# Query and key projections on a PSUM bank each, the first chunk's scores ahead of their second halves, three output biases on VectorE, and a new order of the work

## The chip, the cores and the metric

One core of one Trainium2 chip. The metric is the device time of the kernel in microseconds, the median of three runs. Every time below is in microseconds unless it says ns.

## What is computed

A batch of 32 sequences (B) of 64 tokens (L) with 256 features (D). All of it is float32. Cut to what matters, with the names of the code:

```
y   = x @ Wc[id].T + bc[id]                       # per sequence, 8 subjects
q,k,v = y @ Wq.T + bq, y @ Wk.T + bk, y @ Wv.T + bv    # 16 heads of 16
sim = q k^T / sqrt(16) / (|temperature| + 0.1)    # 64 x 64 per head
s   = sum over 5 frequencies of alpha * sin(2 pi sim / f + phi)
w   = sigmoid(s) / (sum over keys + 1e-10)
o   = (w v) @ Wo.T + bo;  o = layernorm(o) * gamma + beta
x1  = x + o
x2  = layernorm(x1 + relu(x1 @ W1[lang] + b1) @ W2[lang] + b2) * g[lang] + b[lang]
# recurrence over the 32 sequences, its batch the 64 token rows, 256 wide:
c   = sigmoid(f) * c + sigmoid(i) * tanh(g)       # gates from x2 and c
out = x1 + tanh(x2 @ wo.T + c_final @ uo.T + bo)
```

## The kernel before

All engines run lists of calls written out by hand, one list for each engine. Semaphores tie them together. No engine ever takes a later call ahead of an earlier one, so the order of each list sets what a wait holds up.

**Attention.** The 32 sequences are five groups g of 4, 8, 8, 8 and 4. `condition` (L419) makes y, `turn_tokens` transposes it, `conditioned` on VectorE (L1435) adds the bias. `queries` and `keys` (project, L407) make q and k in two chunks c of 128 features (eight heads). Before, chunk c of both q and k goes to PSUM bank c of `pf`: `keys(g, c)` waits on TensorE until ScalarE has copied `queries(g, c)` out (L955). The first chunk of group 0's queries is masked into `qm` by VectorE and ScalarE. All others are spread into it by SP, with eight DMAs each (`spread_q`, L286). `scores` (L479) makes a tile of scores in a bank of `pf`, and `copy_scores` (L982) carries it to SBUF.

The score rows are then worked on in 32 units n. `angle(n, f)` scales a unit for one of five frequencies into int32, partly on VectorE (L1459), partly on ScalarE (L991). `wrap(n)` (L1468, VectorE) takes it modulo a turn. `sines(n)` (L1000, ScalarE) takes all five sines. `add_sine(n, f)` (L1481, L1483, VectorE) sums them with alpha. `weights(n)` (L1006, ScalarE) is the sigmoid. `weighted(n)` (L497, TensorE) multiplies with the values, and `divided(m)` (L1496 to L1500, VectorE) divides two units by their sums. A flag on `sines` and `weights` says that the activation table is to be loaded first (L997, L1004).

**The rest, by eight parts q of four sequences.** `turned`, `output_projection` (L514 the bias as a matmul of a row of ones, L516 the product, weights centred by `centre_output_weights`, L1408 to L1418, so that the mean is zero), `squares` on ScalarE (L1015), a root on GpSimd (L362, L365), `residual` and `residual_added` on VectorE (L1525, L1532), `turn_residual`, `adapter_down` (L530), `hidden` (L1537), `adapter_up` (L538), `base`, `adapted` (L1550), `moments`, the root again, `normalise`, `turn_normed`, `modulated` (L1580) and `shifted_language` (L1586), which makes z ready for the recurrence. SP loads each part's own weights with 13 DMAs (`load_rest`).

**The recurrence.** Step n: `input_gates` (L555) and `state_gates` (L562) on TensorE, `gates` on ScalarE (L1032, then the bias of step n + 2 at L1028), `cell_step` on VectorE (L1591 to L1596), `state_turned` on TensorE (L568), `state_copy` on VectorE (L1601). At the end `state_output`, `output_kept`, `output_part` and `output_sum` gather the eight results, which go through a tanh, a sum and a DMA each.

Of the kernel before, what the change touches and what calls it, by code (L numbers as in the profile page):

```python
# [21 lines left out]
P = 128  # L22
# [55 lines left out]
MASKED_BY_DVE = 5  # L78
BY_PE = (0, 1, 2, 6, 7)
# [34 lines left out]
def build(nc, x_in, xt_in, ids_in, small_in, cond_in, down_in, up_in, up_b_in, rows_in, bo_in, wq_in, wk_in, wv_in, bv_in, wo_in,  # L114
          gate_w_in, gate_u_in, gate_b_in, c0_in, c0t_in, wout_in, uout_in, eye_in, out):
    with ExitStack() as ctx:
# [21 lines left out]
        rows = sb("rows", [P, 3, D])  # L138
# [72 lines left out]
        mask_ready, qm_dve, qm_act = sem("mask_ready"), sem("qm_dve"), sem("qm_act")  # L211
# [45 lines left out]
        def _(sp):  # L257
# [53 lines left out]

            load_cond(1, 1)
            load_cond(1, 0)
# [3 lines left out]
            load_cond(1, 3)  # L317
# [4 lines left out]
            load_cond(2, 2)  # L322
            load_x(2)
            spread_q(1, 1)
            load_cond(2, 3)
            load_cond(2, 1)
            load_rest(1)
            load_cond(3, 1)
            load_cond(3, 3)
            load_cond(3, 2)  # L330
            spread_q(2, 0)
            spread_q(2, 1)
            load_x(3)
            load_rest(2)
            load_cond(3, 0)
            load_x(4)
            load_cond(4, 0)
            load_cond(4, 1)
            spread_q(3, 0)
            load_rest(3)  # L340
            load_rest(4)
            spread_q(3, 1)
# [61 lines left out]
        def _(pe):  # L404
            def project(dst, w, src, oc, n, sem):
                for kc in range(KC):
                    mm = pe.matmul(dst[:, oc, 0:n], w[:, kc, oc * P:(oc + 1) * P], src[:, kc, 0:n],  # L407
                                   start=(kc == 0), stop=(kc == KC - 1))
                mm.then_inc(sem, 1)
# [26 lines left out]
            def queries(g, c):  # L436
                pe.wait_ge(y_ready, g + 1)
                if g == 0:
                    pe.wait_ge(qk_s, 32)
                project(pf, wq, yT, c, SIZES[g] * L, q_done)  # L440

            def keys(g, c):
                pe.wait_ge(q_ready, g * KC + c + 1)
                project(pf, wk, yT, c, SIZES[g] * L, k_done)

            def values(q, h):
# [5 lines left out]
                pe.wait_ge(s_copied, FIRST[g] + SIZES[g] // 2)  # L452
                pvw = pf[:].rearrange("p c (b n) -> p (c b) n", n=P)
# [7 lines left out]
            def scores(n):  # L461
# [3 lines left out]
                if t == 0:  # L465
                    pe.wait_ge(k_ready, g * KC + KC)
# [42 lines left out]
            def output_projection(q, j):  # L509
# [68 lines left out]
            def output_kept(q, j):  # L578
                pe.wait_ge(go_kept, q + 1)
                pe.wait_ge(s_copied, B)  # L580
                pe.wait_ge(att_ready, B // 2)
# [18 lines left out]

            for _ in range(8):
# [9 lines left out]
            queries(0, 1)  # L611
            keys(0, 0)
            keys(0, 1)
# [3 lines left out]
            scores(1)  # L617
            values(0, 0)
# [8 lines left out]
            queries(1, 0)  # L627
            queries(1, 1)
            keys(1, 0)
# [3 lines left out]
            scores(4)  # L633
            scores(5)
            scores(6)
            scores(7)
            weighted(2)
            weighted(3)
            turned(0)
# [18 lines left out]
            adapter_up(0)  # L658
            queries(2, 1)
            keys(2, 0)  # L660
            weighted(4)
            weighted(5)
            turn_normed(0)
            keys(2, 1)
            weighted(6)
            input_gates(0, 0)
            weighted(7)
            input_gates(0, 1)
            input_gates(1, 0)
            state_gates(0)  # L670
            input_gates(1, 1)
            output_part(0, 0)
            output_part(0, 1)
            scores(12)
            scores(13)
            state_turned(0)
            scores(14)
            input_gates(2, 0)
            scores(15)
            state_gates(1)  # L680
            values(3, 0)
            values(3, 1)
            values(4, 0)
            weighted(8)
            weighted(9)
            values(4, 1)
            weighted(10)
            weighted(11)
            input_gates(2, 1)
            input_gates(3, 0)  # L690
            input_gates(3, 1)
            state_turned(1)
            scores(16)
            scores(17)
            turned(1)
            turned(2)
            state_gates(2)
            output_projection(1, 0)
# [3 lines left out]
            output_projection(2, 0)  # L702
            condition(5, 0)
            condition(5, 1)
            condition(6, 0)
            condition(6, 1)
            turn_residual(1)
            output_projection(2, 1)
            state_turned(2)
            adapter_down(1)  # L710
            turn_tokens(3)
            adapter_up(1)
            state_gates(3)
# [3 lines left out]
            turn_normed(1)  # L717
            queries(3, 1)
            input_gates(4, 0)
            state_turned(3)  # L720
            keys(3, 0)
            input_gates(4, 1)
            state_gates(4)
            input_gates(5, 0)
            keys(3, 1)
            turn_residual(2)
            state_turned(4)
            input_gates(5, 1)
            adapter_down(2)
            state_gates(5)  # L730
            weighted(14)
            weighted(15)
            input_gates(6, 0)
            adapter_up(2)
            input_gates(6, 1)
            state_turned(5)
            scores(20)
            scores(21)
            state_gates(6)
            weighted(16)  # L740
            input_gates(7, 0)
            scores(22)
            turn_normed(2)
            state_turned(6)
            input_gates(7, 1)
            state_gates(7)
            scores(23)
            input_gates(8, 0)
            state_turned(7)
            output_part(1, 0)  # L750
            input_gates(8, 1)
# [1368 lines left out]
```

## Time and profile before

| | us |
|---|---|
| median of 3 runs | 362.87 (362.35 to 364.96) |
| the profiled execution's own time | 366.25 |
| its span | 364.5 |
| TensorE, VectorE, ScalarE busy | 305.0, 299.4, 278.6 |
| mean granted TensorE clock, of full speed | 0.963 |

The profile is of one execution, so durations and waits are taken from it. Busy time is not a bound by itself: the stages have different limits. The rows that count are in the section ahead of the prediction. In them a form in brackets behind a row is idle time of that engine just ahead of the row, with what ended it; "issue" stands for time in which nothing the profile shows was waited for. TensorE shows each float32 matmul as two records, so "x8" is four matmuls.

### The profile page before, as it was taken

The page shows a single profiled execution, that of the slowest core. Times are in us where ns is not written, and L with a number is a line of the kernel's source. Part 1 is how long each engine was busy: PE and PEld are TensorE (multiplying, and loading weights), DVE is VectorE, ACT ScalarE, POOL GpSimd, SP SyncE. Part 2 cuts the span into 40 slices and gives each one's busy share as a digit, 9 for nine tenths or more (in the row PEclk, how much of TensorE's full clock was granted, in tenths as well). Part 3 has the DMA queues.
Part 4 walks back from the last instruction along what each step waited for, and adds up shares of the span by engine and source line. Part 5 has one row for each costly group of instructions (what it writes and reads, how often), then busy time and mean ns, then how long its engine had stood idle before and what let it go on. Part 6 is the DMA issues. An engine that isn't in the chain of part 4 may idle for free.

```text
span 364.5 us, 6732 instructions
## 1 busy us (share of the span) xinstructions
PE 305.0 (84%) x2316; PEld 171.6 (47%) x2316; DVE 299.4 (82%) x661; ACT 278.6 (76%) x407; POOL 29.9 (8%) x42
## 2 busy tenths in 40 slices
PE   6947687476898799989888998999987988998895
PEld 5735346244444645534445545444544543543353
DVE  2378974849999999999899999899998999764344
ACT  1387789859999999999989999698995886222223
POOL 6000000001100002220200002000001110101000
PEclk9998699969999789999999999899999999999999
DMA  6448444562610640244123100000332031000006
GB/s 186 154 128 249 178 79 114 153 172 67 182 22 8 137 93 28 55 111 97 31 72 64 14 2 0 2 13 7 77 97 73 3 81 37 3 0 0 2 8 222
DMA packets 31078, 27.52 MB, mean 76 GB/s; under 512 B 11588, under 2 KB 25028, under 8 KB 31045
## 3 DMA queue, kind: packets, MB, share of 16 engines
q1 hardware_dynamic: 30756, 26.58, 27.7%
q10 hardware_dynamic: 288, 0.53, 0.5%
q8 instruction: 18, 0.29, 0.4%
q14 instruction: 16, 0.12, 0.1%
HBM read 23.02 MB, written 2.10 MB: 69 GB/s over the span
## 4 chain that ended last, share of the span: by engine, by line
DVE 48%; PE 20%; issue 11%; ACT 9%; SPq 7%; POOL 2%; DMA 2%; DVEq 0%; ACTq 0%
DVE sc L1483 16%; DVE ang L1468 7%; PE pg L562 4%; DVE ang L1459 4%; PE pf L479 3%; PE pg L555 3%; ACT ang L991 3%; DVE sc L1481 2%; PE pf L407 2%; DVE vz L1449 2%; SPq L286 1%; ACT ang L1000 1%; DVE fc L1591 1%; POOL rs L362 1%; PE pr L573 1%
## 5 line engine op out<-in xcount | busy, mean ns | idle before, releaser
L1483 DVE SCALAR_TENSOR_TENSOR sc<-ang,small,sc 128x512 f32<-128x512 f32 (+1 forms) x160 | 98.2, 639 | 1.5
L1000 ACT ACTIVATE ang<-ang,qs 128x2560 f32<-128x2560 int32 x32 | 77.4, 2426 | 2.6 <-DVE ang L1468 2.3
L991 ACT ACTIVATE ang<-sc,phase 128x512 int32<-128x512 f32 (+1 forms) x126 | 73.3, 642 | 0.3 <-DVE sc L1483 0.2
L555 PE MATMUL pg<-gate_w,zT 128*64 128x384 f32 x256 | 53.5, 520 | 3.3 <-DVE zT L1586 3.3
L1468 DVE TENSOR_SCALAR ang<-ang 128x2560 int32<-128x2560 int32 x32 | 47.4, 1485 | 6.9 <-ACT ang L991 6.7
L562 PE MATMUL pg<-gate_u,cT 128*64 128x384 f32 x256 | 49.0, 504 | 4.0 <-DVE cT L1601 4.0
L479 PE MATMUL pf<-qm,kT 128*64 128x256 f32 x256 | 35.2, 420 | 13.2 <-issue 11.6
L1032 ACT ACTIVATE gat<-pg 128x384 f32<-128x384 f32 x32 | 15.5, 485 | 29.2 <-PE pg L562 28.8
L479 PEld LDWEIGHTS pf<-qm,kT 128*64 128x64 f32 x256 | 19.9, 150 | 25.9 <-issue 16.4
L1459 DVE TENSOR_SCALAR ang<-sc,phase 128x256 int32<-128x256 f32 (+1 forms) x74 | 27.4, 411 | 4.3 <-ACT sc L982 4.3
L562 PEld LDWEIGHTS pg<-gate_u,cT 128*64 128x64 f32 x256 | 16.9, 139 | 25.8 <-issue 16.0
L982 ACT ACTIVATE sc<-pf 128x512 f32<-128x512 f32 x32 | 18.2, 588 | 10.8 <-PE pf L479 10.7
L555 PEld LDWEIGHTS pg<-gate_w,zT 128*64 128x64 f32 x256 | 15.9, 140 | 21.9 <-issue 15.4
L497 PEld LDWEIGHTS pav<-vz,sc 128*64 128x64 f32 x512 | 18.4, 143 | 13.4 <-ACT sc L1006 9.3
L497 PE MATMUL pav<-vz,sc 128*64 128x34 f32 x512 | 20.4, 230 | 5.0 <-ACT sc L1006 3.6
L1006 ACT ACTIVATE sc<-sc 128x512 f32<-128x512 f32 x32 | 19.5, 623 | 2.6 <-DVE sc L1483 2.4
L407 PE MATMUL pf<-yT,wq 128*128 128x512 f32 (+1 forms) x40 | 17.8, 580 | 3.5 <-DVE yT L1435 3.5
L1591 DVE SCALAR_TENSOR_TENSOR fc<-gat,cst 128x128 f32<-128x128 f32 x32 | 9.1, 283 | 13.0 <-ACT gat L1032 13.0
L362 POOL TENSOR_SCALAR rs<-var 128x2 f32<-128x2 f32 x8 | 3.6, 455 | 185.9 <-ACT x L1015 185.9
L457 PE MATMUL pf<-wv,yT 128*64 128x128 f32 x256 | 16.2, 277 | 2.3 <-ACT sc L982 2.3
L1481 DVE TENSOR_SCALAR sc<-ang,small 128x512 f32<-128x512 f32 (+1 forms) x40 | 16.4, 426 | 1.6 <-ACT ang L1000 1.6
L428 PE MATMUL pf<-wc,xg 128*64 128x256 f32 x128 | 14.9, 381 | 2.6 <-issue 1.9
(124 smaller groups left out, 469.3 us busy)
## 6 DMA issues: line engine op xcount, KB each, us to landing
wc<-in_cond SPq DMA_DIRECT2D x30, 257.0 KB, 3.0
wa<-in_down SPq DMA_DIRECT2D x32, 66.0 KB, 1.9
w<-in_up SPq DMA_DIRECT2D x32, 64.2 KB, 2.2
xt<-in_xt SPq DMA_DIRECT2D x8, 256.0 KB, 3.0
b<-in_up_b SPq DMA_DIRECT2D x32, 64.0 KB, 2.1
out_t<-go SPq DMA_DIRECT2D x8, 256.0 KB, 2.3
xg<-in_x SPq DMA_DIRECT2D x3, 512.0 KB, 5.0
qm<-qT SPq DMA_DIRECT2D x48, 32.0 KB, 2.1
```

The source lines that it names most:

```text
L407: mm = pe.matmul(dst[:, oc, 0:n], w[:, kc, oc * P:(oc + 1) * P], src[:, kc, 0:n], start=(kc == 0), stop=(kc == KC - 1))
L479: mm = pe.matmul(dst[u * L:(u + 1) * L, m * PC * L:(m + 1) * PC * L], kT[:, c, b * L:(b + 1) * L], qm[:, b, u, :, :], start=True, stop=True)
L497: mm = pe.matmul(pav[r, col:col + 2 * HV], at[:, b * L:(b + 1) * L], vz[:, b, p, :, :].rearrange("p u d -> p (u d)"), start=True, stop=True)
L555: pe.matmul(pg[n % 2][u * L:(u + 1) * L, 0:GCOLS], zT[:, q % 2, kc, t * L:(t + 1) * L], gate_w[:, kc, u, :], start=False, stop=(kc == KC - ...
L562: mm = pe.matmul(pg[n % 2][u * L:(u + 1) * L, 0:GCOLS], cT[:, kc, :], gate_u[:, kc, u, :], start=False, stop=(kc == KC - 1), skip_group_ch ...
L991: op = act.activation(ang[:, n % SLOTS, f, r], unit(n)[:, r], ACT.Identity, scale=TURN / FREQS[f], bias=phase[:, p * NF + f:p * NF + f + 1])
L1000: act.activation(a.bitcast(F32), a, ACT.Sin, scale=2 * PI_LOW / TURN, bias=qs[:, 3:4]).then_inc(sine_ready, 1)
L1006: act.activation(unit(n), unit(n), ACT.Sigmoid).then_inc(w_ready, 1)
L1459: op = dve.tensor_scalar(ang[:, n % SLOTS, f, r], unit(n)[:, r], TURN / FREQS[f], phase[:, p * NF + f:p * NF + f + 1], ALU.mult, ALU.add)
L1468: dve.tensor_scalar(a, a, (1 << TURN_BITS) - 1, None, ALU.bitwise_and).then_inc(angle_ready, 1)
L1481: op = dve.tensor_scalar(unit(n)[:, r], sine, amp, None, ALU.mult)
L1483: op = dve.scalar_tensor_tensor(out=unit(n)[:, r], in0=sine, scalar=amp, in1=unit(n)[:, r], op0=ALU.mult, op1=ALU.add)
```

## The change

The projections go to a bank each: every query chunk to bank 0 of `pf`, every key chunk to bank 1. `keys(g, c)` no longer waits for the copy of `queries(g, c)`, and each waits for the copy of its own chunk before. In group 0 the scores of the first chunk (units 0 and 1 of the tiles) stand ahead of `queries(0, 1)` and `keys(0, 1)`, and these wait until both are copied out. The key order within a group is q0, k0, q1, k1. For parts 5, 6 and 7 the bias of the output projection is no longer a matmul: VectorE adds a centred row in PSUM (`output_bias`), behind the projection and ahead of `squares`, which waits for it. The row is loaded as a fourth one of `rows` and centred once by `centre_output_row`. `output_kept` waits for the attention's last division for its bank in `pav` alone. `centre_output_weights` moves on VectorE from ahead of the first angles to behind `divided(1)`. The lists of SP, TensorE, ScalarE and VectorE are reordered throughout. ScalarE's has 24 table loads with a flag where it had 20.

```
+SCORES_FIRST = [True] + [False] * (NG - 1)
+BIAS_BY_DVE = (5, 6, 7)
...
             def project(dst, w, src, oc, n, sem):
                 for kc in range(KC):
-                    mm = pe.matmul(dst[:, oc, 0:n], w[:, kc, oc * P:(oc + 1) * P], src[:, kc, 0:n],
+                    mm = pe.matmul(dst[:, 0:n], w[:, kc, oc * P:(oc + 1) * P], src[:, kc, 0:n],
...
             def queries(g, c):
...
-                project(pf, wq, yT, c, SIZES[g] * L, q_done)
+                wait(pe, q_ready, g * KC + c)
+                if c == 1 and SCORES_FIRST[g]:
+                    pe.wait_ge(s_copied, FIRST[g] + SIZES[g] // 2)
+                project(pf[:, 0, :], wq, yT, c, SIZES[g] * L, q_done)
             def keys(g, c):
-                pe.wait_ge(q_ready, g * KC + c + 1)
-                project(pf, wk, yT, c, SIZES[g] * L, k_done)
+                pe.wait_ge(y_ready, g + 1)
+                wait(pe, k_ready, g * KC + c)
+                project(pf[:, 1, :], wk, yT, c, SIZES[g] * L, k_done)
...
             def values(q, h):
...
                 pe.wait_ge(s_copied, FIRST[g] + SIZES[g] // 2)
+                pe.wait_ge(k_ready, g * KC + KC)
...
             def scores(n):
...
-                    pe.wait_ge(k_ready, g * KC + KC)
+                    pe.wait_ge(k_ready, g * KC + (1 if SCORES_FIRST[g] else KC))
...
             def output_projection(q, j):
...
-                if j == 0:
+                own = q in BIAS_BY_DVE
+                if j == 0 and not own:
                     pe.matmul(pr[:, q % 2, :], ones[:, :], bo[:, :], start=True, stop=True)
...
-                                   start=False, stop=(kc == KC - 1), skip_group_check=True)
+                                   start=(own and j == 0 and kc == 0), stop=(kc == KC - 1), skip_group_check=True)
...
             def squares(q):
                 act.wait_ge(o_done, 2 * q + 2)
+                if q in BIAS_BY_DVE:
+                    act.wait_ge(bias_added, BIAS_BY_DVE.index(q) + 1)
...
+            def centre_output_row():
+
+                dve.wait_ge(rest_s, 16 * len(rest_consts))
+                link(dve.tensor_reduce(rowm[:, :], rows[:, 3, :], mybir.AxisListType.X, ALU.add))
+                link(dve.tensor_scalar(rowm[:, :], rowm[:, :], -1.0 / D, None, ALU.mult))
+                dve.tensor_scalar(rows[:, 3, :], rows[:, 3, :], rowm[:, :], None, ALU.add).then_inc(row_centred, 1)
...
+            def output_bias(q):
+                dve.wait_ge(o_done, 2 * q + 2)
+                dve.wait_ge(row_centred, 1)
+                dve.tensor_tensor(tiles(q), tiles(q), row(3), ALU.add).then_inc(bias_added, 1)
```

On TensorE at the start, behind the transposes of group 0, in the kernel before (wq and wk are the weights of queries and keys, qm the masked queries, wv the values' weights):

```order
L407 MATMUL pf<-yT,wq 128x256 x4
L407 MATMUL pf<-yT,wk 128x256 x4
L615 MATMUL pct<-eye 128x128 x3
L479 MATMUL pf<-qm,kT 64x256 x8
L457 MATMUL pf<-wv,yT 64x128 x16
L479 MATMUL pf<-qm,kT 64x256 x8
```

The same place now:

```order
L410 MATMUL pf<-yT,wq 128x256 x2
L410 MATMUL pf<-yT,wk 128x256 x2
L624 MATMUL pct<-eye 128x128 x3
L487 MATMUL pf<-qm,kT 64x256 x8
L410 MATMUL pf<-yT,wq 128x256 x2
L410 MATMUL pf<-yT,wk 128x256 x2
L465 MATMUL pf<-wv,yT 64x128 x16
```

The second half of both projections has moved behind the first eight matmuls of the scores.

On ScalarE, around the weights of units 8 to 11, before (ang is made by the angles and turned into sines, sc<-sc are the weights, gat the gates, sc<-pf the copies of scores):

```order
L997 ACT_TABLE_LOAD
L1000 ACTIVATE ang<-ang,qs 128x2560
L962 ACTIVATE kT<-pf,small 128x512
...
L1000 ACTIVATE ang<-ang,qs 128x2560
L982 ACTIVATE sc<-pf 128x2x4x64 x2
L1000 ACTIVATE ang<-ang,qs 128x2560
L1004 ACT_TABLE_LOAD
L1006 ACTIVATE sc<-sc 128x512
L991 ACTIVATE ang<-sc,phase 128x512
L1006 ACTIVATE sc<-sc 128x512 x2
```

And now:

```order
L1008 ACT_TABLE_LOAD
L1011 ACTIVATE ang<-ang,qs 128x2560 x2
L1045 ACTIVATE gat<-pg 128x384
...
L1015 ACT_TABLE_LOAD
L1017 ACTIVATE sc<-sc 128x512
...
L1008 ACT_TABLE_LOAD
L1011 ACTIVATE ang<-ang,qs 128x2560
...
L1011 ACTIVATE ang<-ang,qs 128x2560
...
L1015 ACT_TABLE_LOAD
L1017 ACTIVATE sc<-sc 128x512
```

Where the three sines of units 9 to 11 shared one load, and the weights of 8 to 11 another, there are now two loads for each.

On VectorE in the tail, from step 22 of the recurrence, before (fc and cst are a step, cT the state's copy, atq the last division, stage the normed tile, zT the part's z):

```order
L1565 TENSOR_SCALAR stage<-b,mv,rs 128x256 x2
L1580 TENSOR_TENSOR zT<-pr,wa 128x512
L1586 TENSOR_TENSOR zT<-zT,wa 128x512
L1591 SCALAR_TENSOR_TENSOR fc<-gat,cst 128x128
L1593 SCALAR_TENSOR_TENSOR fc<-gat 128x128
L1596 SCALAR_TENSOR_TENSOR cst<-fc 128x128
L1601 COPY cT<-pct 128x128
L1519 TENSOR_TENSOR xt<-xt,rows 128x512
L1525 SCALAR_TENSOR_TENSOR x<-pr,rs,rows 128x256 x2
```

And now:

```order
L1590 TENSOR_SCALAR stage<-b,mv,rs 128x256 x2
L1616 SCALAR_TENSOR_TENSOR fc<-gat,cst 128x128
L1618 SCALAR_TENSOR_TENSOR fc<-gat 128x128
L1621 SCALAR_TENSOR_TENSOR cst<-fc 128x128
L1626 COPY cT<-pct 128x128
L1605 TENSOR_TENSOR zT<-pr,wa 128x512
L1611 TENSOR_TENSOR zT<-zT,wa 128x512
L1544 TENSOR_TENSOR pr<-pr,rows 128x512
L1539 TENSOR_TENSOR xt<-xt,rows 128x512
L1616 SCALAR_TENSOR_TENSOR fc<-gat,cst 128x128
L1618 SCALAR_TENSOR_TENSOR fc<-gat 128x128
L1621 SCALAR_TENSOR_TENSOR cst<-fc 128x128
```

Step 22 has moved behind the normed tile of part 6, and the bias of part 7 (pr<-pr,rows) stands ahead of step 23.

## Rows read from the trace of the kernel before

**Rows 1.** Stages: length; PE, PEld, DVE, ACT, POOL busy (count); clock, DMA share, GB/s

```profile
50.00:81.00 31.00, 19.89 (x208) 13.82 (x206) 19.08 (x35) 24.10 (x37) 0.00 (x0) 0.89 0.55 143
81.00:200.00 119.00, 103.56 (x885) 57.99 (x885) 114.01 (x221) 115.48 (x158) 12.49 (x12) 0.97 0.32 75
200.00:280.00 80.00, 73.78 (x556) 39.75 (x556) 77.00 (x167) 72.14 (x105) 6.32 (x10) 0.98 0.13 31
280.00:309.50 29.50, 25.21 (x197) 12.97 (x199) 27.85 (x79) 21.76 (x35) 2.13 (x4) 1.00 0.17 42
```

**Rows 2.** VectorE's waits, 81 to 309.5: in total, times, longest

```profile
DVE ang L1468 <- ACT ang L991: 5.4, 1, 5.4
DVE stage L1565 <- POOL rs L365: 1.5, 2, 0.9
DVE fc L1591 <- ACT gat L1032: 1.4, 1, 1.4
DVE hT L1537 <- PE pr L530: 1.3, 1, 1.3
DVE cT L1601 <- PE pct L568: 0.7, 1, 0.7
```

**Rows 3.** Timeline of the start (start, duration, engine, line, operation)

```profile
13.60 2.00 PE L407 MATMUL pf<-yT,wq 128*128 128x256 f32 x8 [0.19 <-DVE yT L1435]
16.68 0.68 DVE L1408 TENSOR_REDUCE wom<-wo 128x2 f32<-128x512 f32 x1
18.16 1.95 PE L479 MATMUL pf<-qm,kT 128*64 128x256 f32 x16
18.64 0.47 DVE L1418 TENSOR_SCALAR bo<-bo,bom 1x512 f32<-1x512 f32 x1
20.20 6.16 SPq L286 DMA_DIRECT2D qm<-qT  x8
27.73 3.42 PE L479 MATMUL pf<-qm,kT 128*64 128x256 f32 x16 [4.87 <-issue]
```

**Rows 4.** Group 1: chain of waits, timeline, two stretches (columns as rows 1)

```profile
40.79 3.79 PE pf L407 x4
...
45.47 5.13 SPq L286 DMA_DIRECT2D qm<-qT  x8
60.77 2.07 DVE L1459 TENSOR_SCALAR ang<-sc,phase 128x512 int32<-128x512 f32 x5 [1.61 <-ACT sc L982]
74.22 6.14 PE L479 MATMUL pf<-qm,kT 128*64 128x256 f32 x32 [6.74 <-issue]
...
36.00:38.00 2.00, 0.35 (x3) 0.35 (x4) 1.96 (x6) 2.00 (x5) 0.00 (x0) 1.00 0.99 399
42.00:44.00 2.00, 2.00 (x4) 0.80 (x3) 1.96 (x7) 0.31 (x1) 0.00 (x0) 0.50 0.00 0
```

**Rows 5.** VectorE's groups: count, busy us, mean ns

```profile
L1550 DVE TENSOR_TENSOR b<-pr,b 128x512 f32<-128x512 f32 x8 | 5.4, 680 | 0.0
```

**Rows 6.** Timeline of the tail, TensorE and VectorE

```profile
314.49 1.12 PE L514 MATMUL pr<-bo,ones 1*128 1x512 f32 x2
325.76 0.87 PE L555 MATMUL pg<-gate_w,zT 128*64 128x384 f32 x4
341.12 0.29 DVE L1591 SCALAR_TENSOR_TENSOR fc<-gat,cst 128x128 f32<-128x128 f32 x1 [2.13 <-ACT gat L1032]
344.79 0.29 DVE L1591 SCALAR_TENSOR_TENSOR fc<-gat,cst 128x128 f32<-128x128 f32 x1 [2.13 <-ACT gat L1032]
```

**Rows 7.** Timeline of ScalarE around a table load

```profile
226.28 0.20 ACT L1015 ACTIVATION_READ_ACCUMULATOR x<-pr 128x1 f32 x1
226.50 1.28 ACT L997 ACT_TABLE_LOAD   x1
227.79 2.43 ACT L1000 ACTIVATE ang<-ang,qs 128x2560 f32<-128x2560 int32 x1
```

**Rows 8.** SP's last issue for part 5 (timeline)

```profile
279.51 0.47 SPq L278 DMA_DIRECT2D b<-in_up_b  x1
```

More of the change, by code:

```diff
@@ L617, in _ @@
             scores(1)
+            queries(0, 1)
+            keys(0, 1)
             values(0, 0)
@@ L717, in _ @@
             turn_normed(1)
-            queries(3, 1)
[L719 to L723, printed above, removed]
+            keys(3, 0)
+            turn_residual(2)
+            input_gates(4, 0)
+            input_gates(4, 1)
+            output_part(1, 0)
+            adapter_down(2)
+            state_gates(4)
+            output_part(1, 1)
+            adapter_up(2)
+            queries(3, 1)
+            weighted(14)
@@ L858, in _ @@
+            input_gates(18, 1)
+            state_turned(17)
+            turned(6)
+            adapter_down(5)
+            state_gates(18)
+            adapter_up(5)
+            output_kept(1, 0)
+            output_projection(6, 0)
+            output_projection(6, 1)
+            state_turned(18)
+            weighted(28)
+            input_gates(19, 0)
+            input_gates(19, 1)
+            weighted(29)
             turn_normed(5)
+            state_gates(19)
+            turn_residual(6)
@@ L1078, in _ @@
             angle(0, 3)
+            queries(0, 1)
             angle(0, 4)
-            sines(0, True)
+            keys(0, 1)
             angle(1, 3)
             angle(1, 4)
+            sines(0, True)
+            sines(1, False)
             copy_scores(2)
@@ L1206, in _ @@
             angle(16, 4)
-            sines(15, True)
-            gates(3)
             queries(3, 0)
-            sines(16, False)
+            sines(15, False)
+            residual_turned(2)
+            weights(14, True)
+            keys(3, 0)
             angle(17, 1)
@@ new lines, in _ @@
+            add_sine(21, 3)
+            state_copy(8)
+            add_sine(21, 4)
+            angle(23, 0)
+            angle(24, 0)
+            angle(24, 1)
+            wrap(22)
+            base(3)
+            hidden(3)
+            wrap(23)
+            adapted(3)
+            cell_step(9)
+            wrap(24)
+            divided(10)
+            moments(3)
+            add_sine(22, 0)
+            add_sine(22, 1)
+            state_copy(9)
+            add_sine(22, 2)
+            normalise(3)
@@ L1974, in _ @@
+            hidden(5)
+            add_sine(29, 4)
+            angle(30, 1)
+            angle(31, 0)
+            adapted(5)
+            cell_step(18)
+            moments(5)
+            output_bias(6)
+            wrap(30)
+            normalise(5)
+            state_copy(18)
+            shifted(6)
+            residual(6)
             modulated(5)
-            angle(31, 0)
+            residual_added(6)
             shifted_language(5)
             angle(31, 1)
+            cell_step(19)
```

951 lines of the change are left out of this document (450 added, 501 removed).

## Prediction

> **What bounds the kernel now.** I read the stages first, then VectorE's waits, then the three places where the change moves something. The stages [rows 1] show one long saturated stretch, from 81 to the end of the last sine sum at 309.5. In it VectorE is busy 114.01 + 77.00 + 27.85 = 218.9 of 228.5 us, and ScalarE 115.48 + 72.14 + 21.76 = 209.4. The reader is to see these two columns. So VectorE sets the pace and ScalarE is close behind: 3.5 us idle in the first 119, 7.9 in the next 80, 7.7 in the last 29.5. From 50 to 81 VectorE is idle for 11.9 of 31 us. Behind 309.5 follows a tail of 55 us, in which the recurrence and the chain of the last part run beside each other.
>
> Of VectorE's 9.6 idle us between 81 and 309.5 the waits [rows 2] name 1.5 (for GpSimd's root), 1.4 (gates), 1.3 (the adapter's first product) and 0.7 (the turned state), 4.9 together; three more come to 1.2. The rest, 3.5, is gaps between instructions. (The 5.4 in that view lies ahead of 81.) This is the first bound: work on VectorE there does not shrink, so whatever the new orders do, that stretch can win 6.1 us at most, less what the change adds.
>
> **The start.** Before, both queries, both keys and their four copies stand ahead of the first scores, which begin at 18.16 [rows 3]. Now one projection of each suffices. The row at 13.60 holds both query projections in 2.00, so one less is 1.0, and the keys' likewise. With its own bank the key's first projection runs without waiting for the query's copy, and ScalarE has one query and one key fewer to copy ahead of the scores. ScalarE's masks stay in the way, so I take 0.9 earlier and not more. The second half pays: its queries wait until the first scores are copied out (19.9) and take 1.0, their copy ends at about 21.4. SP's spreading of them began at 20.20 [rows 3]; now it begins at 21.4, and the scores of units 2 and 3, 7.5 behind it before (27.73), at 28.9. That is 1.2 late. VectorE does not notice, since the new order gives it units 0 and 1 whole meanwhile. What follows is a chain: the next group's first query projection (40.79, 3.79 us), its copy, SP's spreading of it (45.47). ScalarE now runs the sines of unit 1 ahead of scores 2, so the token copies that feed this chain are not later, and the vector step ahead of it ends about 0.4 earlier by VectorE's work (two units of 4.2 us from 28.2, then 1.1 and 1.5 us). The granted clock in 42 to 44 is 0.50, that is 1.2 GHz; TensorE had been busy for 0.35 of the 2 us from 36 to 38, ahead of the fall [rows 4]. At 2.4 GHz the projection would take half, 1.9 less. I leave it at the lower level.
>
> From that spreading to the scores of unit 8 at 74.22 SP's queue is full: 28.75 us from 45.47 [rows 4], the same issues in the same number in the new order. ScalarE stands behind those scores with its copies, and VectorE waits 5.4 for it [rows 2]. So all the VectorE idle time before 81 hangs on one number, when 45.47 comes, and I move it by 0.5. VectorE does some more sine sums ahead of the wait now (1.4) and waits some 0.8 longer behind it, for the squares of part 0: 0.6 gained. Term: **-1.1**, of which I count -0.6, since the first half of it stands on ends that I worked out to a few tenths. Ends: -3.0 (the higher clock too) and +1.2 (the late second scores pass on).
>
> The centring of the output weights (16.68 to 19.11, 2.43 us [rows 3]) leaves the gap ahead of the first angles and goes behind the second division. There VectorE waits 1.61 for scores [rows 4], and the division itself comes some 2.5 earlier, since its product now stands ahead of scores 5 to 7. Cost 0; if that cover is gone, 2.4.
>
> **VectorE's added work.** Two of the three biases, for parts 5 and 6, fall before the last sine sum. The nearest operation reads the same PSUM tiles and adds a tile: 680 ns [rows 5], so 1.36. It writes SBUF; nothing here shows one that writes PSUM. Ends 0.5 and 1.2 each; I take 0.68. Centring the bias row is three of the seven instructions of the weights' centring [rows 3], one of them on half the width: 0.7 to 2.4, taken 1.0. One state copy (0.2) goes behind the last sine sum. Term: **+2.2**. TensorE loses three bias products of 1.12 [rows 6], two of them in a stretch where it is not the bound.
>
> **The new orders.** Where they take a wait away it is named: the gates' 1.4, the adapter's 1.3 and the state's 0.7 [rows 2]. Steps 1 to 3 of the recurrence now stand 12 to 28 us of VectorE's work earlier, and steps 4 to 19 have more of other work between them; I count those 3.4 as gone. The 1.5 for the root stays: behind the moments of parts 1 and 2 stand now 1.0 and 1.6 us of other work, before 2.1 and 2.1, and even that did not cover it. Term: **-3.4**.
>
> ScalarE pays for this: 24 table loads in place of 20, one pair more in units 8 to 11 and one in 22 to 25. A load takes 1.28 [rows 7], so four take 5.1. The first pair, 2.6, goes into the stretch up to 200 where ScalarE has 3.5 idle, the second into one with 7.9 [rows 1]. The sines of late units stand 4 to 5 us of ScalarE's work further back, their first sums on VectorE 1 to 2 us further. Ends: 0 (all in idle time) and 5.1 (all passed on). Taken: half of the first pair, nothing of the second. Term: **+1.3**.
>
> Here a rule speaks against the change. Between the accumulator read that ends at 226.48 and the load at 226.50 lies no gap, and the sine starts 0.01 behind the load [rows 7]: a switch costs 1.28. The Trainium skill (ScalarE: Activation LUTs, What ACT_TABLE_LOAD costs) puts a drain of 1.38 us beside each load, 2.66 together. By it the four would be 10.6. The trace disagrees with it, with its 0.02 us.
>
> **The last parts.** The tail has the same ten steps of the recurrence. Part 7 sets its end as much as they do: its normed tile is ready just when step 28 needs it, and from there each step takes 3.67 (341.12 to 344.79 [rows 6]). For part 7 the bias product (1.12) leaves, and a VectorE operation (0.7 and a semaphore) stands between the projection and the squares instead: these start 0.4 earlier. Then the new VectorE order costs: the residual of part 7 stands behind step 23 and its copy, which wait for gates that ScalarE does behind the squares. Counted from the end of the last sine sum, with the durations of before: squares to +8.5, gates 23 to +9.0, step 23 to +9.8, its turned copy to +10.6, residual and sum to +12.15; before that was +11.6. Next hidden(7) to +15.2, state_gates(25) to +16.0, input_gates(26, 0), 0.87 long [rows 6] and now ahead of adapter_up(7), to +16.7, the product to +17.7, the copy of state 25 and the sum of part 7 to +19.0; before +17.3. Step 26 (+21.5) waited for gates before too and takes 1.0 of it up: the normed tile and its two operations (z) end at +24.4, before +23.65. Behind the last step TensorE's work is the same in another order. Term: **+0.7**, ends -0.6 and +2.
>
> **The sum.** -0.6 + 2.2 - 3.4 + 1.3 + 0.7 = +0.2. The profiled execution took 366.25 us (span 364.5 and 1.75 around it), 3.4 above the median of the runs; against its own time the sum is 366.4, and as a difference on the median 362.87 it gives 363.1.
>
> **Rivals.**
> (A) The orders win nearly all that can be won: the 6.1 us of waits go, the loads hide in ScalarE's idle time, and the projection at 40.79 finds the clock at 2.4 GHz (1.9). For it: VectorE's named waits are few, and the recurrence has more room. Against it: ScalarE needs 118 of the 119 us up to 200. -0.6 - 1.9 + 2.2 - 6.1 + 0 + 0 = -6.4: 356.5.
> (B) ScalarE becomes the bound, which is slower. Its four loads all reach VectorE, each as a wait of a first sine sum for its sines, in units 8 to 27. It decides once ScalarE's own idle time between 81 and 280 falls under some 3 us in place of 11.4. Then the gates come late as well and VectorE's waits stay: -0.6 + 2.2 + 5.1 + 0.7 = +7.4: 370.3. With one pair passed on, 367.7. For it: 3.5 idle in 119 is little, and keys(3, 1) and the queries and keys of the last group come 5 to 11 us of ScalarE's work later. Those feed SP: behind scores 28 and 29 SP does the last spreading and then the loads of two parts without a break, to 279.51 [rows 8], and the adapter's wait of 1.3 [rows 2] is for these. If those scores are 2 late, it is 3.
> (C) The orders do nothing: as many waits come as go. -0.6 + 2.2 + 1.3 + 0.7 = +3.6: 366.5.
> (D) A switch stops ScalarE for longer than its load, wherever work is in flight. No row shows it; if each of the four cost its 1.28 twice, that would be 5.1 on top of B, 375.4. The drain of the page named above is such a stop.
>
> **Chances and range.** Around the forecast (359.5 to 366), 0.46; A or most of it, 0.29; B, 0.15; C, 0.08; D, 0.02. A measurement of this kernel can tell about 1%, 3.6 us. Faster than 359.3 is A, 0.29. Slower than 366.5 is B, D and three quarters of C, 0.23. Within is the rest, 0.48. The range takes in A and most of B: 355.5 to 369.5. The forecast's own is 360 to 366.5.
>
> **What would show it.** First scores near 17.3 and those of unit 2 near 29. The scores of unit 8 within 1 us of 73.7. ScalarE's idle time from 81 to 280 at 5 to 8 us; near 2 it is B. VectorE's waits for sines at units 8 to 27 under 2 in sum. The bias additions at 0.7. Steps 22 to 27 of the recurrence within 1 us of 24.2 in all, from the last sine sum on, and 3.67 behind that. I am wrong if the last sine sum ends before 305 or behind 314.

## The result and the profile after

| | us |
|---|---|
| changed kernel, median of 22 runs | 367.94 (363.16 to 369.87) |
| kernel before, median of 22 runs | 363.67 (361.39 to 366.3) |
| ratio | 1.0106 (95%: 1.0083 to 1.0129) |
| profiled execution of the changed kernel, span | 368.23, 366.4 |

The change costs 1.06%, some 3.9 us, just more than what a measurement of this kernel can tell. Ratios leave disturbed runs out, medians don't, so one can say a little more than the other.

One thing has to be known before the traces are compared. The profiled execution of before (366.25) was 2.6 above its median, that of after 0.3 above. So the traces differ by 1.9 us where the runs differ by 4.3.

The stages after, in the columns of [rows 1]:

```profile
50.00:81.00 31.00, 22.66 (x213) 15.76 (x213) 22.86 (x45) 25.36 (x41) 0.93 (x2) 0.83 0.46 132
81.00:200.00 119.00, 101.23 (x884) 58.05 (x880) 113.11 (x216) 117.72 (x153) 6.75 (x10) 0.99 0.27 74
200.00:280.00 80.00, 71.95 (x548) 38.74 (x549) 76.39 (x167) 74.64 (x113) 7.70 (x10) 0.98 0.13 34
280.00:311.50 31.50, 26.06 (x211) 13.40 (x207) 29.61 (x85) 19.81 (x32) 2.59 (x4) 1.00 0.17 45
```

The last sine sum ends at 311.4, before at 309.5. From 81 to there VectorE is idle 11.4 us (230.5 less 219.1), before 9.6. Ahead of 81 it is the other way round: 27.5 idle of 81 (53.46 busy), before 29.4 (51.61 busy). Added up to the last sine sum, VectorE is idle as long as before (38.9 and 39.0), and busy 272.5 in place of 270.5, the size of the added work. ScalarE has 1.3 idle in the first 119 us, before 3.5. VectorE's waits in that stretch, which answer to [rows 2]:

```profile
DVE sc L1494 <- ACT ang L1011: 1.8, 2, 1.1
DVE xt L1539 <- DMA xt<-in_xt: 1.7, 1, 1.7
DVE b L1570 <- DMA b<-in_up_b: 1.5, 1, 1.5
DVE yT L1448 <- PE pf L418: 1.4, 1, 1.4
DVE rden L1509 <- PE pav L505: 0.8, 1, 0.8
DVE stage L1590 <- POOL rs L368: 0.6, 1, 0.6
```

The gates' 1.4, the adapter's 1.3 and the state's 0.7 are gone, as forecast. In their place stand two waits for loads, 3.2 together, and three others, 4.0 together: for sines (1.8), for the condition's turned product (1.4) and for the weighted values (0.8). The chain of waits leads to the loads (start, duration, what; many pieces are left out):

```profile
258.56 1.32 DVE sc L1496 x2
259.88 0.61 DVE zT L1611
264.26 0.76 SPq L279
265.20 0.68 SPq L280
281.76 2.09 DMA b<-in_up_b
283.88 0.69 DVE b L1570
```

The chain of the end runs from VectorE into SP's queue and comes out some 23 us later. SP's rows behind the last spreading, whose issues end at 258.97 (SP's timeline; L275 is the first issue of a part's load):

```profile
260.51 0.40 SPq L275 DMA_DIRECT2D xt<-in_xt  x1
...
271.43 0.59 SPq L275 DMA_DIRECT2D xt<-in_xt  x1
...
281.76 0.47 SPq L281 DMA_DIRECT2D b<-in_up_b  x1
```

The load of part 6 stands ahead of that of part 5, and it overwrites buffers of part 4. It waits for `shifted_language(4)` on VectorE, which ends at 260.48. Before, that step ended at 251.9, six us ahead, and the load of part 6 began at 258.03, when the spreading ended. The load of part 5 needs nothing so late, but stands behind: the end of the loads is at 282.2 in place of 280.0 [rows 8]. VectorE meets it twice (the last column of [rows 5] and here: idle time just ahead):

```profile
274.39 0.69 DVE L1539 TENSOR_TENSOR xt<-xt,rows 128x512 f32<-128x512 f32 x1 [1.69 <-DMA xt<-in_xt]
...
283.88 0.69 DVE L1570 TENSOR_TENSOR b<-x,b 128x512 f32<-128x512 f32 x1 [1.48 <-DMA b<-in_up_b]
```

TensorE at the start, to be held against [rows 3]:

```profile
17.22 1.95 PE L487 MATMUL pf<-qm,kT 128*64 128x256 f32 x16 [0.82 <-ACT kT L973]
19.95 1.10 PE L410 MATMUL pf<-yT,wq 128*128 128x256 f32 x4 [0.79 <-ACT sc L993]
...
29.08 3.68 PE L487 MATMUL pf<-qm,kT 128*64 128x256 f32 x16 [4.16 <-issue]
33.50 5.81 PE L431 MATMUL pf<-wc,xg 128*64 128x256 f32 x32 [0.73 <-issue]
...
42.90 1.98 PE L410 MATMUL pf<-yT,wq 128*128 128x512 f32 x4 [1.32 <-DVE yT L1448]
```

The condition product of group 1 (L431) before:

```profile
31.88 3.68 PE L428 MATMUL pf<-wc,xg 128*64 128x256 f32 x32 [0.73 <-issue]
```

It now takes 2.1 longer, with the granted clock at 0.50 from 28 to 36 (before at 0.51 to 0.63 from 28 to 32, then at full). The query projection behind it begins 2.1 later than before (42.90, before 40.79) and takes 1.98 in place of 3.79, at the full clock. SP's spreading begins at 45.78, before at 45.47.

VectorE's added work is as sized (groups by line):

```profile
L1544 DVE TENSOR_TENSOR pr<-pr,rows 128x512 f32<-128x512 f32 x3 | 2.1, 692 | 0.1
```

### The profile page after: what moved, and what is told of

Same layout as the page of the kernel before. It is cut to its first block, busy times and chain, and to the rows that moved or that the text cites. A ratio compares the mean times of both kernels' runs of the same rounds, so it can differ in the third digit from the quotient of the medians.

```text
span 366.4 us, 6770 instructions
## 1 busy us (share of the span) xinstructions
PE 303.4 (83%) x2310; PEld 172.1 (47%) x2310; DVE 302.7 (83%) x667; ACT 283.8 (77%) x411; POOL 27.0 (7%) x42
## 4 chain that ended last, share of the span: by engine, by line
DVE 47%; PE 18%; ACT 15%; issue 10%; SPq 6%; DMA 2%; POOL 1%; DVEq 0%; ACTq 0%
DVE sc L1496 16%; DVE ang L1481 5%; DVE ang L1472 4%; ACT ang L1002 4%; PE pf L487 4%; ACT ang L1011 3%; DVE sc L1494 3%; PE pg L571 2%; PE pf L431 2%; PE pr L525 2%; DVE fc L1616 1%; PE pf L465 1%; DVE fc L1618 1%; DVE vz L1462 1%; DVE cst L1621 1%
## 5 line engine op out<-in xcount | busy, mean ns | idle before, releaser
L564 PE MATMUL pg<-gate_w,zT 128*64 128x384 f32 x256 | 50.7, 499 | 2.0 <-ACT pg L1041 1.1
L571 PE MATMUL pg<-gate_u,cT 128*64 128x384 f32 x256 | 47.9, 495 | 4.7 <-DVE cT L1626 4.7
L487 PE MATMUL pf<-qm,kT 128*64 128x256 f32 x256 | 36.0, 426 | 12.3 <-issue 7.5
L505 PE MATMUL pav<-vz,sc 128*64 128x34 f32 x512 | 19.6, 227 | 3.0 <-DVE atq L1513 2.3
L465 PE MATMUL pf<-wv,yT 128*64 128x128 f32 x256 | 19.3, 311 | 3.3 <-ACT sc L993 2.1
L410 PE MATMUL pf<-yT,wq 128*128 128x512 f32 (+1 forms) x40 | 16.2, 527 | 4.5 <-DVE yT L1448 3.7
L465 PEld LDWEIGHTS pf<-wv,yT 128*64 128x64 f32 x256 | 17.0, 158 | 6.1 <-ACT sc L993 4.0
L431 PE MATMUL pf<-wc,xg 128*64 128x256 f32 x128 | 17.7, 423 | 2.6 <-issue 1.5
```

Of the source, the lines that this page charges most:

```text
L431: mm = pe.matmul(pft[row:row + L, j, :], xg[:, kc, b * L:(b + 1) * L], wc[:, b, kc * D:(kc + 1) * D], start=(kc == 0), stop=(kc == KC - 1))
L465: mm = pe.matmul(pvw[u * L:(u + 1) * L, b, :], yT[:, kc, b * L:(b + 1) * L], wv[:, kc, u, :], start=(kc == 0), stop=(kc == KC - 1))
L487: mm = pe.matmul(dst[u * L:(u + 1) * L, m * PC * L:(m + 1) * PC * L], kT[:, c, b * L:(b + 1) * L], qm[:, b, u, :, :], start=True, stop=True)
L505: mm = pe.matmul(pav[r, col:col + 2 * HV], at[:, b * L:(b + 1) * L], vz[:, b, p, :, :].rearrange("p u d -> p (u d)"), start=True, stop=True)
L564: pe.matmul(pg[n % 2][u * L:(u + 1) * L, 0:GCOLS], zT[:, q % 2, kc, t * L:(t + 1) * L], gate_w[:, kc, u, :], start=False, stop=(kc == KC - ...
L571: mm = pe.matmul(pg[n % 2][u * L:(u + 1) * L, 0:GCOLS], cT[:, kc, :], gate_u[:, kc, u, :], start=False, stop=(kc == KC - 1), skip_group_ch ...
```

## The experiments

Every ratio is to the kernel before, run on the same chip in turn. A per cent is 3.6 us.

**1. The SP pair and the bias work.** After the traces there were two accounts of the loss: VectorE's added 2.1 us (theory W), or the loads (theory Q). The first run leaves the bias of parts 5 to 7 with TensorE:

```diff
-BIAS_BY_DVE = (5, 6, 7)
+BIAS_BY_DVE = ()
```
and without `output_bias` and `centre_output_row` on VectorE.

> The changed kernel with the bias product of all parts back on TensorE; VectorE's three bias additions and the centring of the row are gone. Theory W (the slowdown is VectorE's added work, 2.1 us up to the last sine sum, in a stretch that VectorE bounds): 2.1 to 2.9 us under the changed kernel, so +1.5 to +2.2 against the kernel before, and VectorE's busy time up to the last sine sum back at 270.5. Theory Q (the work goes into waits; what costs is the load of two parts' vectors behind the last spreading on SP's queue): within 0.7 us of the changed kernel, the waits of VectorE on the loads at 274 and 284 as long or longer.

Measured: 1.0122 (1.0063 to 1.0181), no faster than the changed kernel. The wait at the loads went from 1.69 to 1.79, and VectorE, busy 1.7 less up to the last sine sum (270.8), is idle 2.8 more (41.7): the work taken away turned into waiting. One of the new waits, 1.8, is for a product of the adapter on TensorE, which has its three bias products (1.12 each) back. So this run prices an exchange between two engines and not VectorE's work alone, and so do the next two on the bias. The second run swaps two lines of SP's list:

```diff
+            load_rest(5)
             load_rest(6)
-            load_rest(5)
```

> The changed kernel with one pair on SP's queue swapped: the load of part 5's vectors ahead of part 6's, whose wait for the turned vector of part 4 (released at 260) holds it up. Theory Q: VectorE's waits at shifted(5) (1.69 us) and base(5) (1.48) go, so 2.5 to 3.2 us under the changed kernel, +1.0 to +1.8 against before. Theory W: other waits take their place (for ScalarE's sines and gates, which are no earlier), within 0.7 us of the changed kernel, and the two waits reappear elsewhere within 20 us.

Measured: 0.9975 (0.9931 to 1.0018), 1.3% under the changed kernel (by the two ratios 4.8 us, give or take 1.8). Both waits are gone, and the only new one is 0.7 for the gates:

```profile
269.44 0.68 DVE L1539 TENSOR_TENSOR xt<-xt,rows 128x512 f32<-128x512 f32 x1
...
277.37 0.68 DVE L1570 TENSOR_TENSOR b<-x,b 128x512 f32<-128x512 f32 x1
```

Theory Q holds and W falls. The trace gives 3.3 of the 4.8: from the end of the first sine sum of unit 28 to the last of unit 31 it is 35.4 us in place of 38.7.

With both edits the bias work should have shown, since its cover was gone.

> The changed kernel with both edits: part 5's vectors loaded ahead of part 6's, and all bias products on TensorE. With the waits for the loads gone, VectorE's 2.1 us of bias work should now show: 1.5 to 2.5 us under the run with the swap alone (362.15), so about 360 and -0.7% against before. Rival (the bias work was never on the path, the first run's 0 being its true price): within 0.7 us of 362.15.

Measured: 0.9987 (0.996 to 1.0015), so moving the bias work back to TensorE brings nothing there, within 1.9 us; the rival of that run was right. The bias alone on the kernel before:

> The kernel before with the bias change alone: same banks and orders, three bias additions and the row's centring on VectorE, three bias products fewer on TensorE. Theory W: +1.8 to +2.6 us against before (0.7 + 0.7 + about 0.7 up to the last sine sum, and -0.4 to +0.4 in the tail). Rival (it goes into VectorE's waits): within 0.5 us of before. Each bias addition 0.68 to 0.70 us.

Measured: 1.0033 (0.9988 to 1.0078). This allows anything from -0.4 to 2.8 and doesn't tell W's 1.8 to 2.6 from the rival's 0. All three runs together speak for well under 2 for the exchange. What VectorE's 2.1 us would cost without the products that leave TensorE, no run shows.

**2. The same swap in the kernel before.**

> The kernel before with part 5's vectors loaded ahead of part 6's, the pair swapped that was worth 5 us in the changed kernel. There the load of part 6 held the queue for 1.5 us only in theory (its release came before the spreading ended), and VectorE waited 0.45 + 1.35 us on the loads of part 5. Theory Q: these 1.8 us go, -1.0 to -1.8 against before. Rival (the swap is worth its 5 us in any order, as part 5 no longer stands behind 9.7 us of issues): -3 or more. If other waits hide it: within 0.5.

Measured: 0.9937 (0.9891 to 0.9982), -2.3 us: the small waits on part 5's loads were there before too. So of the swap's 4.8 the new orders brought about 2.5 (give or take 2.4), and the rest was an old debt. This is the fastest kernel by its ratio. It beats the kernel before and the changed one; from the changed kernel with the swap (0.9975) it is not told apart.

**3. The table loads.** Four more loads in the kernel before, by turning the flag of `sines` and `weights` of units 10 and 25 to True:

> The kernel before with four more loads of ScalarE's table and nothing else: ahead of the sines of units 10 and 25 and of the weights of units 10 and 25, 24 loads in place of 20, each of a table that is in already. Theory L (ScalarE has no room, its loads reach VectorE): +2.5 to +5.1 us against before. Theory W and my forecast's term (the first pair half, the second hidden): +0.5 to +1.5. If a load of the table in place is cheaper than 1.28 us, the run says nothing on the loads of the change.

Measured: 1.0148 (1.0092 to 1.0205), +5.4. A load of the table in place costs as much as another:

```profile
L997 ACT ACT_TABLE_LOAD x12 | 15.4, 1283 | 0.2
```

Theory L holds by the runs: four loads are 5.1 us, and 5.4 (3.3 to 7.4) reached the end. In the trace the first sine sums stand 0.4 behind those of before at unit 8, ahead of the loads, 2.8 at unit 14 and 3.3 at unit 31. So there the first pair (unit 10) passes on 2.4 of its 2.6, and the second (unit 25) some 0.4: 2.8 in all, and what the runs have above that is not placed. The Trainium skill (ScalarE: Activation LUTs, What ACT_TABLE_LOAD costs) puts 2.66 us, a drain of 1.38 included, on every switch to a different set, and names no price for a set that is in place. With 2.66 each the four would be 10.6, outside the interval. The 24 loads of the changed kernel are all such switches, and in its trace each has 0.02 us of idle time ahead of it and, but for one (0.38), 0.01 behind it, with no room for that drain on ScalarE.

In the changed orders, with the swap, one pair more:

> The changed kernel with part 5's vectors loaded first and one more pair of table loads (of the table in place, ahead of the sines and the weights of unit 11; 26 loads). Theory L (ScalarE bounds up to unit 28 in the new orders too): +2.0 to +2.6 us against the run with the swap alone (0.9975 of before), so 1.003 to 1.005. Rival (the new orders leave ScalarE room, the loads are hidden there, the loss of the run with one pair less was of another kind): within 0.7 us of it.

Measured: 1.018 (1.0126 to 1.0234), +7.4 against the swap alone (give or take 2.5): far over the 2.6 of two loads, which no theory of mine had. The trace shows where. Against that of the swap alone the first sine sum is 2.4 behind at unit 10, ahead of the loads, 4.9 at unit 12, 8.2 at unit 14, and so it stays to the end: 5.8 for the pair. TensorE's stretches in this run (columns as [rows 1]):

```profile
134.00:138.00 4.00, 4.00 (x9) 1.96 (x9) 3.96 (x5) 3.97 (x5) 0.00 (x0) 0.50 0.00 0
138.00:142.00 4.00, 4.00 (x17) 2.13 (x18) 3.94 (x9) 1.92 (x3) 0.00 (x0) 0.50 0.00 0
142.00:146.00 4.00, 4.00 (x26) 1.99 (x23) 0.77 (x2) 3.04 (x3) 0.00 (x0) 0.83 0.01 4
```

The swap alone:

```profile
134.00:138.00 4.00, 4.00 (x25) 2.03 (x23) 3.96 (x8) 4.00 (x8) 0.00 (x0) 1.00 0.02 4
138.00:142.00 4.00, 2.97 (x17) 1.88 (x17) 3.90 (x8) 3.98 (x9) 1.21 (x2) 1.00 0.00 0
```

Behind the later weights TensorE is busy 2.46 us of 4 in 130 to 134 (in the run with the swap alone 4.00), its granted clock falls to 0.50, ScalarE then waits 3.0 for its scores and VectorE 3.2 for the sines behind them:

```profile
145.91 0.49 DVE L1494 TENSOR_SCALAR sc<-ang,small 128x512 f32<-128x512 f32 x1 [3.23 <-ACT ang L1011]
```

The same products, at 1.2 GHz, are late. Whether the clock or the order behind it has the larger part is not told apart here.

The other way round, a pair fewer:

```diff
-            weights(8, True)
...
-            weights(9, False)
...
-            sines(10, True)
+            sines(10, False)
...
+            weights(8, True)
+            weights(9, False)
...
-            weights(10, True)
+            weights(10, False)
```
(both behind `sines(11, False)`, with `gates(2)` after them)

> The changed kernel with part 5's vectors loaded first, and one pair of table loads fewer: on ScalarE the weights of units 8 and 9 go behind the sines of units 10 and 11, so the loads ahead of sines(10) and weights(10) go (22 in place of 24). Theory L (each load of the table reaches the end, as four did in the kernel before: 5.5 us): -2.0 to -2.7 us against the run with the swap alone (362.15). Rival (the pair was put there because the early weights feed the work behind them; without it VectorE waits for the products): 0 or slower, up to +2.

Measured: 1.0316 (1.0276 to 1.0356), +12 against the swap alone. The loads saved are not seen: TensorE waits 8.5 us for the weights of unit 8, and both other engines wait for what it has behind them (VectorE 7.7, ScalarE 5.4).

```profile
118.00:122.00 4.00, 0.00 (x0) 0.00 (x0) 0.00 (x0) 3.98 (x5) 0.00 (x0) 0.65 0.32 80
```
```profile
123.52 1.92 PE L505 MATMUL pav<-vz,sc 128*64 128x34 f32 x32 [8.49 <-ACT sc L1017]
```

So this pair of loads is the price of weights that come early, and TensorE's and VectorE's new lists are written for them. The run says nothing on what a load costs; it says that the pair can't be taken out alone.

**4. The start.** The banks everywhere and group 0's first scores ahead, the rest in the orders of before, but for two things: `turn_residual(2)` stands ahead of `keys(3, 1)` on TensorE, and ScalarE's copies of group 0's second chunks stand between its first angles. VectorE's order is that of before, so it is not given units 0 and 1 whole:

> The kernel before with the change of the start alone: the banks, and group 0's first scores ahead of its second projections (on ScalarE the two second copies behind the first angles), everything behind in the orders of before. My forecast: first scores 0.9 earlier, scores 2 1.2 later, -0.6 in the whole, within 1 us of before. Rival (the chain from the spreading to scores 2 passes its lateness on, as the changed kernel's second spreading, 1.3 late, showed): +0.5 to +1.5. Rival (the whole gain of the first scores passes on): -1.

Measured: 1.0214 (1.0165 to 1.0263), +7.8, under no theory. Most of it has a cause of its own. With a bank by kind, `keys(3, 1)` waits for the copy of `keys(3, 0)`, and on ScalarE that copy stands late:

```profile
169.18 2.80 PE L410 MATMUL pf<-yT,wk 128*128 128x512 f32 x4 [3.59 <-ACT kT L973]
```
```profile
172.23 0.29 DVE L1626 COPY cT<-pct 128x128 f32<-128x128 f32 x1 [4.09 <-PE pct L577]
```

Behind the stopped keys on TensorE stands a turned state, VectorE waits for it 4.1 (6.7 with a second wait for one), and ScalarE 4.2 for VectorE. The new bank scheme removes one wait (a key for its query's copy) and adds another (a key for the key ahead of it); the new orders space the copies for it (in the changed kernel's trace no projection waits for a key's copy from 140 to 200). The next run keeps the old banks from group 1 on:

```diff
-                project(pf, wk, yT, c, SIZES[g] * L, k_done)
+                project(pf[:, 1 if g == 0 else c, :], wk, yT, c, SIZES[g] * L, k_done)
```
and likewise for the queries.

> The kernel before with the change of the start alone, and with the banks by kind in group 0 only: the groups behind keep a bank per chunk, so keys(3, 1) does not wait for the copy of keys(3, 0), which held TensorE for 3.6 us and both other engines for 4 in the run with banks by kind everywhere. If that wait was the whole loss of that run (8.6 us), this one is within 1 us of before: my forecast's term for the start is -0.6. Rival (the start itself costs: scores 2 come 1.2 later and ScalarE's masks stay in the way): +1 to +2, and +8 if the start was the whole loss.

Measured: 1.0078 (1.0041 to 1.0114), +2.8. The start itself costs, in the orders of before. In this trace scores 2 begin at 29.62, and VectorE's sums of unit 1, at 37.68 in the profile of before, move to:

```profile
39.83 1.80 DVE L1492 SCALAR_TENSOR_TENSOR sc<-ang,small,sc 128x256 f32<-128x256 f32 x4
```

Over the profiles the shift is steady: scores 2 begin at 27.3 to 28.4 in the four with the old start and nothing else added there, and at 28.5 to 29.6 in the eight with the new one, though their first scores come 1 earlier. By scores 8 (71.1 to 74.6 against 72.4 to 74.2) it is hidden in what the clock does, so the 2.8 is known as a whole and is traced only up to unit 3.

The changed kernel gives VectorE other work at the start, so these two runs don't price the start there. Its trace, and those of the five runs in its orders, show this much: VectorE is idle 7.6 to 8.8 us from 12.8 to 50 (in the four profiles with the old start and nothing added there 4.9 to 7.4), and 7.7 to 9.0 from 50 to 81 (9.5 to 11.9). So it does notice the later second scores, and by 81 the rest of the new orders has made up for it.

**5. The clock of the first 80 us.** Runs of one kernel spread by 7 us, and the ends of the spread go with the mean granted clock: of the 23 runs of before beside those of the swap in it, those at 0.979 or more took 359.1 to 360.5, those at 0.962 took 362.6 to 365.8. (Lower still, at 0.955, three took 363.4 to 364.5.) In most profiles the clock falls somewhere between 26 and 46, between 52 and 66 and between 70 and 80, the first and the last behind idle stretches of TensorE. So I filled two of these on top of the swap in the kernel before:

```diff
+            for _ in range(24):
+                pe.matmul(pct[:, :], eye[:, :], eye[:, :], start=True, stop=True)
             scores(2)
...
+            for _ in range(27):
+                pe.matmul(pct[:, :], eye[:, :], eye[:, :], start=True, stop=True)
             scores(8)
```

> The kernel before with part 5's vectors loaded first, and TensorE kept busy in two idle stretches of about 4 us with products of the identity into a tile that nobody reads (24 ahead of scores(2), 27 ahead of scores(8), 0.14 us each). In the profiles the granted clock falls to 0.50 in 28 to 36 and 72 to 78, behind these stretches, and runs of one kernel spread by 8 us with their mean clock. Theory K (that spread and some us of the time are these falls): the falls go, the mean clock is at 0.975 or more in all runs, -1.5 to -3.5 us against the run with the swap alone (0.9937 of before), and the runs spread by less than 3 us. Rival (VectorE and ScalarE have other work meanwhile, or the clock falls elsewhere): within 0.7 us of it, spread as before.

Measured: 1.0005 (0.9969 to 1.0041), 0.7% above the swap alone (give or take 0.6); theory K missed. The mean clock was 0.976 to 0.993, and the runs spread by 4.3 us. But I had counted records for products, so each took 0.23 us in place of the 0.14 I wrote:

```profile
23.49 5.62 PE L621 MATMUL pct<-eye 128*128 128x128 f32 x48
29.05 1.95 PE L479 MATMUL pf<-qm,kT 128*64 128x256 f32 x16
```

With 14 and 15 products:

> As the run with 24 and 27 products of the identity, with 14 and 15. There each product took 0.117 us twice (48 records in 5.62 us), so the first set ended at 29.1, 1.7 behind the time at which scores(2) began without it (27.34), and the second at 73.3, 1.2 behind; the granted clock stayed at 1.00 all the same. 14 products are 3.3 us and 15 are 3.5, in gaps of 3.9 and 4.1. Theory K (the falls of the clock cost some us and only the delays ate the gain): the clock stays up, scores(2) begin by 27.5, -1.0 to -2.5 us against the run with the swap alone (0.9937 of before). Rival (VectorE and ScalarE have other work while TensorE runs at the lower level): within 0.7 us of it.

Measured: 0.9978 (0.9927 to 1.0029), median 361.02 beside 364.71 for before; the swap alone had 361.61 beside 363.68. The two lie within each other's uncertainty (by the ratios this one is 1.5 us worse, by the medians 1.6 better), and the gain K asked for isn't shown. Scores 2 began at 27.90, not by 27.5. The second fill held the clock at 1.00 from 70 to 78. The first held it to 36, and then it fell in another place, ahead of the queries of group 1:

```profile
28.00:36.00 8.00, 5.75 (x48) 3.61 (x48) 7.93 (x18) 6.53 (x12) 0.00 (x0) 1.00 0.80 232
36.00:44.00 8.00, 5.11 (x13) 2.71 (x14) 7.83 (x18) 5.81 (x10) 0.00 (x0) 0.69 0.67 256
```
The swap alone, same stretches:
```profile
28.00:36.00 8.00, 7.27 (x37) 4.08 (x34) 7.59 (x17) 6.19 (x11) 0.00 (x0) 0.50 0.86 243
36.00:44.00 8.00, 5.51 (x29) 3.07 (x26) 7.39 (x16) 7.00 (x12) 0.00 (x0) 1.00 0.64 238
```

The runs did draw together (359.0 to 364.0, the swap alone 358.4 to 365.6), on another chip and by less than K had asked.

## Why the prediction was right and wrong

The time, 367.94, lies in the range (355.5 to 369.5) and 4.8 above the forecast of 363.1, outside the forecast's own 360 to 366.5. "Within 1%" was the likeliest, and the ratio is 1.06% slower. So the sum was wrong, and that the range held is in part luck: it is 14 us wide, and terms that were too small (the loads, SP's queue) stand against a price and a gain that were misjudged the other way. Yet every tell that I had named came true: first scores at 17.22, those of unit 2 at 29.08, of unit 8 at 73.37; ScalarE idle 6.6 us from 81 to 280; waits for sines 1.8; bias additions 0.69; step 27 ends 25 behind the last sine sum, then 3.67 a step; the last sine sum at 311.4. They were too weak: all could hold and the kernel still be 1% slower. And they were set against one profile of before that was itself 2.6 above its median.

- **The start (-0.6).** In the orders of before it is wrong in sign: +2.8 (1.5 to 4.1). The first scores and the lateness of scores 2 were right to 0.2 us. In the changed kernel its price is not measured, but two steps failed there. "VectorE does not notice": it is idle 8.8 from 12.8 to 50, before 6.9. And "the token copies that feed this chain are not later": the condition product took 5.81 in place of 3.68 at the lower clock, and SP's spreading began 0.3 later and not 0.5 earlier. The 1.9 that rival A hoped for from the clock at the query projection did come (1.98 in place of 3.79) and made up for most of that.
- **VectorE's added work (+2.2).** Its size was right (0.69 each, three times, and the row's centring in 0.9), its price was too high for the exchange as a whole: by three runs well under 2, and in the new orders none that could be measured (within 1.9). I had argued that work on a saturated engine must reach the end. That the 10 us of idle time between its waits took it in is argued; the products that left TensorE may have paid for it as well.
- **The new orders (-3.4).** The three named waits went, and five others came, 7.2 together, two of them for loads. What I had put under rival B, the load of two parts behind the last spreading, came from another side: not late scores but a later release of part 6's load. It cost 3.2 in waits and about 2.5 net. The step that failed is that I read SP's queue only for when its issues end [rows 8], and not for what each waits for.
- **The four table loads (+1.3).** Undersized. In the kernel before four cost 5.4, in the new orders one pair more cost 7.4. "Half of the first pair" is the step that failed: it took ScalarE's idle time as room, and in the trace that pair passed on 2.4 of its 2.6. "Nothing of the second" was nearly right there (0.4). The change's own four loads were not priced alone in its orders.
- **The last parts (+0.7).** From the last sine sum to the end of step 31 it is 39.8 us in both, to within 0.1.

If the parts add up, start, bias, loads and SP's queue make 2.8 + 0 + 5.4 + 2.5 = 10.7, and the change costs 3.9. The rest of the orders would then win about 7, near rival A's 6.1 of waits and more than my 3.4. This is a remainder, not a measurement: no run has the new orders without the rest, the 2.8 and the 5.4 were measured in the orders of before, and the two runs on the pair of loads show that the parts don't simply add.

Of the rivals none is the whole of it. C gave 366.5, B with one pair 367.7, and the time lies beside these. B's mechanism (loads of the table reach VectorE) is shown in the kernel before; in the changed one VectorE waits 1.8 for sines, and B's sign, ScalarE idle for near 2 us, did not appear. C's, as many waits as before, is what VectorE's idle time shows. D is not shown: in the kernel before four loads cost their own length, and beside the 24 switches of the changed kernel there is no idle time on ScalarE that would show a stop.

## What to carry to other kernels

When an order is changed, look at each queue for the first item whose release has moved behind the time at which the queue reaches it, and at who stands behind that item: here two swapped lines were worth about as much as the whole change cost (4.8 and 3.9). Price work added to a "saturated" engine by trying it, not by its length, and the same for extra instructions on the engine that feeds it: of two equal pairs one passed on 2.4 us and the other 0.4. And before traces are compared, see how far each profiled execution lies from the median of its runs.

## What the runs showed of the hardware

A table load of the table in place costs 1.283 us, as any other. Two such loads cost 7.4 us in one order, and four cost 5.4 in another. In the trace of the first TensorE runs short of work, its granted clock falls to 0.50, and the products behind it run at 1.2 GHz. The ends of the spread between runs, 7 us at one and the same program, go with the mean granted clock, and two profiles show the fall at different places (28 to 32 and 38 to 46 in one, 26 to 36 in another, whose program is the same up to there). Filling an idle stretch kept the clock up in it; in one profile of two the fall came ten us later instead, and no gain in time was measured.
